# The first recurrence: a norm in pieces of 32 tokens, and the bias as a row of ones

## The reference

```python
residual = x
h = x.transpose(0, 2, 3, 1).reshape(Bsz, Hh * Ww, C)
mu = jnp.mean(h, axis=-1, keepdims=True)
var = jnp.mean((h - mu) ** 2, axis=-1, keepdims=True)
hn = (h - mu) * jax.lax.rsqrt(var + LN_EPS) * gamma + beta
z = jnp.einsum('blc,ec->ble', hn, W_in) + b_in
u = jnp.einsum('ble,se->bls', z, Bm)
def step(state, u_t):
    state = jnp.tanh(state @ A.T + u_t)
    return (state, state)
_, states = jax.lax.scan(step, init, u_tm)
y = jnp.einsum('bls,es->ble', states, Cm) + z * D
out = jnp.einsum('ble,ce->blc', y, W_out) + b_out
return out + residual
```

## Time and profile before

| | us |
|---|---|
| median of 3 runs | 684.7 (683.07 to 684.82) |
| the profiled execution | 685.12 |
| its span | 683.3 |
| TensorE busy | 483.1 |
| ScalarE busy | 324.3 |
| VectorE busy | 300.2 |

### The profile page before, as it was taken

One profiled execution on the slowest core, in us unless ns is written; L12 is line 12 of the kernel. 1 busy time (PEld: TensorE's weight loads), 2 busy tenths in 40 slices (PEclk: granted clock), 3 DMA queues, 4 the chain that ended last, 5 costly groups with the idle time before them and its releaser, 6 DMA issues.

```text
span 683.3 us, 10793 instructions
## 1 busy us (share of the span) xinstructions
PE 483.1 (71%) x3952; PEld 267.9 (39%) x3953; DVE 300.2 (44%) x721; ACT 324.3 (47%) x1093; POOL 8.6 (1%) x11
## 2 busy tenths in 40 slices
PE   4654555556797589999856666666667799989753
PEld 2221222223563466766623333333332454446311
DVE  1184000005983678888843000000007888378533
ACT  3232333333672757777732333333347555666433
POOL 0000000000000000000000000000003000000010
PEclk9655555556999999999995555555559999999867
DMA  5000000000000000000000000000003110000000
GB/s 195 0 2 1 0 1 1 0 1 0 0 2 1 0 2 1 1 1 1 2 0 1 0 1 0 1 1 0 1 0 85 38 39 6 1 2 3 0 9 33
DMA packets 8381, 7.44 MB, mean 11 GB/s; under 512 B 3202, under 2 KB 8066, under 8 KB 8196
## 3 DMA queue, kind: packets, MB, share of 16 engines
q1 hardware_dynamic: 8324, 6.70, 3.3%
HBM read 4.99 MB, written 0.52 MB: 8 GB/s over the span
## 4 chain that ended last, share of the span: by engine, by line
PE 57%; DVE 16%; ACT 16%; issue 7%; DVEq 1%; DMA 1%; SPq 1%; ACTq 0%
PE ps L325 17%; ACT arena L343 11%; PE ps L303 4%; PE ps L308 3%; PE ps L672 2%; PE ps L879 2%; PE ps L842 2%; PE ps L659 2%; PE ps L655 2%; PE ps L858 2%; PE ps L686 2%; DVE arena L1411 2%; DVE arena L1420 2%; PE ps L846 2%; PE ps L265 2%
## 5 line engine op out<-in xcount | busy, mean ns | idle before, releaser
L325 PE MATMUL ps<-arena,wsb 16*16 16x16 f32 (+1 forms) x1024 | 131.1, 206 | 116.9 <-ACT arena L343 111.4
L343 ACT ACTIVATE arena<-ps 16x16 f32<-16x16 f32 (+1 forms) x512 | 96.0, 188 | 191.0 <-PE ps L325 191.0
L325 PEld LDWEIGHTS ps<-arena,wsb 16*16 16x16 f32 (+1 forms) x1024 | 76.2, 118 | 200.3 <-ACT arena L343 186.9
L349 DVE TENSOR_TENSOR X<-X,ps 128x128 f32<-128x128 f32 x16 | 4.6, 287 | 199.3 <-PE ps L308 199.3
L1103 ACT ACTIVATE arena<-ps,arena 128x128 f32<-128x128 f32 (+1 forms) x128 | 52.3, 418 | 31.2 <-DVE arena L1412 31.1
L1211 ACT ACTIVATE arena<-ps 128x512 f32<-128x512 f32 x72 | 40.8, 595 | 26.8 <-PE ps L846 24.3
L1560 DVE TENSOR_TENSOR arena<-arena,ps 128x512 f32<-128x512 f32 x64 | 42.0, 682 | 17.3 <-ACT arena L1211 13.5
L1411 DVE TENSOR_REDUCE arena<-ps 128x2 f32<-128x512 f32 (+1 forms) x48 | 33.0, 688 | 18.7 <-PE ps L655 11.2
L672 PE MATMUL ps<-wsb,arena 128*128 128x128 f32 x192 | 30.4, 282 | 13.5 <-DVE arena L1420 13.5
L659 PE MATMUL ps<-arena 128*128 128x256 f32 x128 | 34.8, 395 | 0.0
L1420 DVE TENSOR_TENSOR arena<-arena 128x512 f32<-128x512 f32 x48 | 33.2, 691 | 1.6
(11 more groups left out here) (277 smaller groups left out, 753.4 us busy)
## 6 DMA issues: line engine op xcount, KB each, us to landing
wsb<-weights SPq DMA_DIRECT2D x1, 2060.5 KB, 9.4
arena<-w SPq DMA_DIRECT2D x20, 64.0 KB
arena<-xn SPq DMA_DIRECT2D x9, 128.0 KB, 2.5
wsb<-weights SPq DMA_DIRECT2D x1, 549.5 KB, 4.4
X<-x SPq DMA_DIRECT2D x1, 512.0 KB, 3.4
out<-arena SPq DMA_DIRECT2D x2, 256.0 KB, 2.4
arena<-w_biases SPq DMA_DIRECT2D x20, 17.0 KB
csb<-consts SPq DMA_DIRECT2D x1, 128.0 KB, 9.2
```

The source lines that it names most:

```text
L325: nc.tensor.matmul(step_columns(k, rows, r), w_state, states[0:rows, :, :, t].rearrange("p g j -> p (g j)"), start=False, stop=True, skip_ ...
L343: nc.scalar.activation(states[0:rows, :, :, t + 1].rearrange("p g j -> p (g j)"), step_columns(t // STEP_BANK, rows, t % STEP_BANK), func) ...
```

## The change

Ahead of step 0 only the first 32 tokens of each sequence are normalised (128 columns in place of 1024), with ScalarE as before. The other seven pieces of 32 tokens are normalised during the recurrence: TensorE centres a piece with 4 products (`chunk_products`, L335 in the changed kernel) and sums squares with 4 more (L340), each behind one step, at the steps that CENTRED and VARIED list; VectorE does the rest, with 1/sigma from an integer start value and three Newton steps (L1347 to L1359), since ScalarE keeps the tanh. The bias no longer goes through VectorE: `states` gets a 17th row of ones, the state matrix a_w a 17th row that holds Bm by the bias of z (L598, L599). The skip product is made bank by bank behind the steps r = 5, 8, 11, 14 (`skip_product`, L320), one step behind the out product (L311) that it waits for, and the last piece's at r = 20, 23, 26, 29 of the last bank. The fills move from r = 17, 20, 23, 26 to 20, 23, 26, 29, in the second recurrence too. The mask tables on VectorE stand behind the seventh piece. The first layer's weights come in two DMAs.

```diff
+FILLS, OUTS, SKIPS = (20, 23, 26, 29), (4, 7, 10, 13), (5, 8, 11, 14)
+CENTRED = ((0, 1, 2, 3), (16, 17, 18, 19), (32, 33, 34, 35), (49, 50, 51, 53), (65, 66, 67, 70), (85, 86, 88, 89), (105, 108, 111, 112))
+VARIED = ((6, 7, 8, 9), (24, 25, 27, 28), (41, 44, 47, 48), (59, 60, 62, 63), (80, 81, 82, 83), (94, 95, 98, 99), (117, 118, 120, 121))
...
-            if g == G - 1:
-                mm.then_inc(s["bank out"], 1)
+            mm.then_inc(s["bank out"], 1)
+
+        def skip_product(pe, m, g):
+
+            group = slice(C * g, C * (g + 1))
+            bank, c0 = (m, P) if m < BANKS - 1 else (m - 1, 2 * P)
+            pe.wait_ge(s["bank out"], G * bank + g + 1)
+            nc.tensor.matmul(ps[group, bank, c0:c0 + P], g2[group, group], xnj[group, :, STEP_BANK * m:STEP_BANK * (m + 1)],
+                             start=True, stop=True).then_inc(s["L0 skip"], 1)
+
+        def chunk(t, m):
+
+            return t.rearrange("p (j t) -> p j t", j=J)[:, :, STEP_BANK * m:STEP_BANK * (m + 1)]
+
+        def chunk_products(pe, t):
+
+            for m in range(1, BANKS):
+                for g in range(G):
+                    group = slice(C * g, C * (g + 1))
+                    if t == CENTRED[m - 1][g]:
+                        if g == 0 and m > 2:
+                            pe.wait_ge(s["L0 chunk saved"], 2 * (m - 2))
+                        nc.tensor.matmul(ps[group, 4 + m % 2, 0:P], W("centre")[group, group], chunk(X[:], m)[group], start=True, stop=True)\
+                            .then_inc(s["L0 chunk products"], 1)
+                    if t == VARIED[m - 1][g]:
+                        if g == 0:
+                            pe.wait_ge(s["L0 chunk saved"], 2 * m - 1)
+                        nc.tensor.matmul(ps[group, 6 + m % 2, 0:P], W("block")[group, group], chunk(sq[:], m)[group], start=True, stop=True)\
+                            .then_inc(s["L0 chunk products"], 1)
...
-                if r == 0 and n == 0:
-                    pe.wait_ge(s["bank biased"], k + 1)
-                if r == 0 and n == 1:
+                if r == 0:
                     pe.wait_ge(s["bank filled"], fills(n, k, G))
...
-                nc.tensor.matmul(step_columns(k, rows, r), w_state, states[0:rows, :, :, t].rearrange("p g j -> p (g j)"),
+                nc.tensor.matmul(step_columns(k, rows, r), w_state, states[0:rows + ones, :, :, t].rearrange("p g j -> p (g j)"),
...
-                if k > 0 and r in (4, 7, 10, 13):
-                    bank_out(k - 1, (r - 4) // 3, rows, w_out)
-                if k < BANKS - 1 and r in (17, 20, 23, 26):
-                    if n == 0 and k + 1 == 6 and r == 17:
-
-                        pe.wait_ge(s["L0 skip added"], 2)
-                    if n == 1 and STEP_BANK * (k + 1) == P and r == 17:
+                if n == 0 and k == 1 and r == OUTS[0]:
+                    pe.wait_ge(s["L0 weights"], 2)
+                if k > 0 and r in OUTS:
+                    bank_out(k - 1, OUTS.index(r), rows, w_out)
+                if n == 0 and k > 0 and r in SKIPS:
+                    skip_product(pe, k - 1, SKIPS.index(r))
+                if n == 0 and k == BANKS - 1 and r in FILLS:
+                    skip_product(pe, k, FILLS.index(r))
+                if n == 0:
+                    chunk_products(pe, t)
+                if k < BANKS - 1 and r in FILLS:
+                    if n == 0 and r == FILLS[0]:
+
+                        pe.wait_ge(s["L0 chunk saved"], 2 * (k + 1 if k < 3 else min(k + 3, BANKS - 1)))
+                    if n == 1 and STEP_BANK * (k + 1) == P and r == FILLS[0]:
                         pe.wait_ge(s["F input"], 2)
-                    bank_fill(pe, n, k + 1, (r - 17) // 3, rows, w_in)
+                    bank_fill(pe, n, k + 1, FILLS.index(r), rows, w_in)
...
-            sp.dma_start(wsb[:, 0:l0], weights[:, 0:l0]).then_inc(s["L0 weights loaded"], 16)
+            norm = COL["L0_W_in"][0]
+            sp.dma_start(wsb[:, 0:norm], weights[:, 0:norm]).then_inc(s["norm weights loaded"], 16)
+            sp.dma_start(wsb[:, norm:l0], weights[:, norm:l0]).then_inc(s["L0 weights loaded"], 16)
             sp.dma_start(wsb[:, l0:], weights[:, l0:]).then_inc(s["weights loaded"], 16)
...
+            pe.wait_ge(s["x loaded"], 16)
+            pe.wait_ge(s["norm weights loaded"], 16)
+            nc.tensor.matmul(ps[:, 7, 0:P], W("centre"), chunk(X[:], 0), start=True, stop=True).then_inc(s["centred"], 2)
             pe.wait_ge(s["L0 weights loaded"], 16)
-            nc.tensor.matmul(ps[:, 4, 0:P], W("L0_W_in", E2), W("L0_BmT", E2), start=True, stop=True)
-            nc.tensor.matmul(ps[:, 4, P:2 * P], W("L0_Cm", E2), W("L0_W_outT", E2), start=True, stop=True)
             nc.tensor.matmul(ps[0:E2, 5, 0:1], W("L0_W_inT", C), W("L0_beta", C), start=True, stop=True).then_inc(s["L0 folds"], 1)
-            pe.wait_ge(s["L0 z bias"], 1)
-            nc.tensor.matmul(ps[:, 4, 2 * P:3 * P], W("L0_W_in", E2), d_wout[:], start=True, stop=True)
-            nc.tensor.matmul(ps[:, 5, 2:3], W("L0_BmT", E2), z_b[:], start=True, stop=True)
-            nc.tensor.matmul(ps[:, 5, 1:2], d_wout[:], z_b[:], start=True, stop=True).then_inc(s["L0 folds"], 1)
-
-            norm_tensor(pe, 0)
+            pe.wait_ge(s["squares"], 2)
+            nc.tensor.matmul(ps[:, 6, 0:P], W("block"), chunk(sq[:], 0), start=True, stop=True).then_inc(s["variance"], 2)
+            nc.tensor.matmul(ps[:, 4, 0:P], W("L0_W_in", E2), W("L0_BmT", E2), start=True, stop=True).then_inc(s["L0 folds"], 1)
+            pe.wait_ge(s["L0 z bias"], 2)
+            nc.tensor.matmul(ps[0:NS + 1, 3, 0:NS], W("ident", NS)[:, 0:NS + 1], W("L0_AT", NS)[:, 0:NS], start=True, stop=False)
+            nc.tensor.matmul(ps[0:NS + 1, 3, 0:NS], z_row, W("L0_BmT", E2)[:, 0:NS], start=False, stop=True).then_inc(s["L0 folds"], 1)
+            nc.tensor.matmul(ps[:, 2, 0:P], W("L0_Cm", E2), W("L0_W_outT", E2), start=True, stop=True)
+            nc.tensor.matmul(ps[:, 2, P:2 * P], W("L0_W_in", E2), d_wout[:], start=True, stop=True)
+            nc.tensor.matmul(ps[:, 2, 2 * P:2 * P + 1], d_wout[:], z_row[:, NS:], start=True, stop=True).then_inc(s["L0 folds"], 1)
             pe.wait_ge(s["L0 weights"], 1)
             pe.wait_ge(s["normalised"], 2)
             for g in range(G):
-                bank_fill(pe, 0, 0, g, NS, u_w[:])
-
-            for h in range(2):
-                nc.tensor.matmul(ps[:, 6 + h, :], g2[:], halves(xn)[h], start=True, stop=True).then_inc(s["L0 skip"], 1)
-            recur_tensor(pe, 0, NS, u_w[:], W("L0_AT", NS)[:, 0:NS], g1[0:NS, 0:C])
+                mm = nc.tensor.matmul(ps[0:NS, 0, g * P:(g + 1) * P], u_w[:, C * g:C * g + NS], chunk(xn[:], 0),
+                                      start=(g == 0), stop=True, skip_group_check=True)
+            mm.then_inc(s["bank filled"], G)
+            pe.wait_ge(s["X ready"], 1)
+            recur_tensor(pe, 0, NS, u_w[:], a_w, g1[0:NS, 0:C], ones=1)
             pe.wait_ge(s["weights loaded"], 16)
+            pe.wait_ge(s["L0 chunk saved"], 2 * (BANKS - 1) + 1)
...
-            norm_scalar(act, 0)
+            act.preload_act_table_set(EXP_LN)
+            act.wait_ge(s["centred"], 2)
+            nc.scalar.activation(chunk(sq[:], 0), ps[:, 7, 0:P].rearrange("p (j t) -> p j t", j=J), ACT.Square, scale=C ** -0.5)\
+                .then_inc(s["squares"], 2)
+            act.wait_ge(s["variance"], 2)
+            nc.scalar.activation(chunk(sq[:], 0), ps[:, 6, 0:P].rearrange("p (j t) -> p j t", j=J), ACT.Ln, bias=W("eps"))\
+                .then_inc(s["log variance"], 2)
+            act.wait_ge(s["log variance"], 2)
+            nc.scalar.activation(chunk(sq[:], 0), chunk(sq[:], 0), ACT.Exp, scale=-0.5).then_inc(s["1/sigma"], 2)
...
-            dve.wait_ge(s["x loaded"], 16)
-            nc.vector.memset(states[:, :, :, 0:1], 0.0).then_inc(s["X ready"], 1)
+            nc.vector.memset(z_row, 0.0)
+            link(nc.vector.memset(states[0:NS + 1], 1.0))
+            nc.vector.memset(states[0:NS, :, :, 0:1], 0.0).then_inc(s["X ready"], 1)
...
-
-            def bias_bank(k):
-
-                dve.wait_ge(s["bank filled"], fills(0, k, G))
-                nc.vector.tensor_scalar(ps[0:NS, k, :], ps[0:NS, k, :], u_b[0:NS], None, ALU.add).then_inc(s["bank biased"], 1)
-
-            bias_bank(0)
-            for h in range(2):
-                dve.wait_ge(s["L0 skip"], h + 1)
-                nc.vector.scalar_tensor_tensor(halves(X)[h], ps[:, 6 + h, :], o_b[:], halves(X)[h], ALU.add, ALU.add)\
-                    .then_inc(s["L0 skip added"], 1)
-            dve.wait_ge(s["L0 skip added"], 2)
-            bias_bank(1)
...
+            dve.wait_ge(s["L0 folds"], 3)
+            nc.vector.tensor_copy(a_w, ps[0:NS + 1, 3, 0:NS]).then_inc(s["L0 weights"], 1)
+            dve.wait_ge(s["1/sigma"], 2)
+            nc.vector.tensor_tensor(chunk(xn[:], 0), chunk(sq[:], 0), ps[:, 7, 0:P].rearrange("p (j t) -> p j t", j=J), ALU.mult)\
```

(34 more changed lines are left out.)

27 lines of the change are left out of this document (13 added, 14 removed).

## The result

The changed kernel took 677.07 us, median of 4 executions (676.33 to 677.42), against 684.51 for the kernel before on the same chip (683.07 to 684.82): a ratio of 0.9877, 95% interval 0.9845 to 0.9909. It is faster by 7.4 us (1.2%), where 15.2 were forecast, and outside the range of 666 to 674.5. The profiled execution took 676.94 us, its span is 675.0 (before 685.1 and 683.3).

What follows compares the result with a forecast made beforehand. The two recurrences, closed chains of steps, were taken to bound the kernel, with 22.2 us ahead and 5.1 inside. 685.1 - 11.2 - 5.1 + 1.5 + 0.3 - 0.9 = 669.7, 0.4 lower for the median: 669.3 us; range 666 to 674.5.

Steps and rivals of the forecast that it cites:

- step 64: Inside the first recurrence: step 64 no longer waits for VectorE's bias, 0.60 instead of 5.72 us, gain 5.1 us.
- VectorE's chain: Normalising pieces on VectorE during the recurrence: 13 dependent operations plus copy and squares per piece, cost 0.3 us (0 to 1.0).
- start: Ahead of the first recurrence: step 0 at 11.0 us instead of 22.2, gain 11.2 us (10.0 to 12.2).
- skip waits: Recurrence steps behind 28 waiting skip products: 0.16 us each for 7, 0.02 for 21, cost 1.5 us (0 to 8.4).
- clock: TensorE in the recurrence: a third of the 1.2 us from the upper clock level, plus lessened skip cost, gain 0.9 us.
- Rival C: Clock goes up and stays: no skip cost, 1.2 us from steps, start 1.0 earlier, 666.5 us; chance 0.13.
- From the end of the recurrence on, each stage as long as before: Sign for everything behind the first recurrence: no stage there changes its length.
- both tight places: Pieces 3 to 4 and 5 to 6, steps 59 and 94: no wait at 0.32 us per operation, 0.4 each at 0.352.
- Rival B: Skip products hold a recurrence step whole: 8.4 us in place of 1.5, no clock gain, 677 us; chance 0.10.
- D: Each of 88 new products behind steps pushes the next step by 0.21 us: costs 18.5, total 686.9; chance 0.03.
- E: Step 64's wait returns elsewhere: VectorE operations at 0.45 us, pieces late, some 8 to 10 us, 678 us; chance 0.04.

Runs made afterwards that it cites:

- e3: The kernel before with only the mask tables' loop on VectorE split around the bias of bank 2: 680.15 us, ratio 0.9913.
- e2: The changed kernel with the 28 skip products two steps behind their out product instead of one, seven chunk products a step earlier: 671.28 us, ratio 0.9815.
- e6: The kernel before with 88 already met waits added to TensorE's program, ahead of three waits it has anyway: 693.84 us, ratio 1.0112.
- e12: The changed kernel without TensorE's implied wait for the saved copy three units back, 45 instructions fewer: 674.85 us, ratio 0.9820.
- e4: The changed kernel with the 2060.5 KB transfer of the other weights issued only once the first layer's weights are there: 677.22 us, ratio 0.9896.
- e1: The changed kernel with the first layer's weights in one DMA again: 674.77 us, ratio 0.9849.
- e11: The kernel before with 88 empty waits in TensorE's program, one behind each of 88 first-recurrence steps from step 139: 694.86 us, ratio 1.0158.
- e5: The changed kernel with 168 already met waits added to TensorE's program, ahead of three waits it has anyway: 677.38 us, ratio 0.9891.
- e7: The changed kernel with later skip products, large weights after the first layer's, piece 4's first two variance products a step later, 168 empty waits: 673.14 us, ratio 0.981.
- e10: The changed kernel with later skip products, delayed large weights, later chunk 4 variances, and 160 empty waits behind recurrence steps: 674.87 us, ratio 0.9863.
- e14: The kernel before without TensorE's implied wait for the saved copy three units back, 45 instructions fewer: 685.24 us, ratio 0.9981.
- e9: The changed kernel with 160 empty waits in TensorE's program, two behind each of 80 first-recurrence steps from step 128: 680.56 us, ratio 0.9966.

## Why the prediction was wrong

Of the mechanisms it named, step 64 and VectorE's chain came as priced, the start and the skip waits were mis-sized, and the clock's gain didn't come; one cost it didn't have. Forecast against measured, in us:

| term | forecast | measured | from |
|---|---|---|---|
| start | -11.2 | -9.65 | step 0 at 12.55 |
| step 64 | -5.1 | -5.1 | ordinary step; e3 alone -5.06 |
| 28 waits of skip products | +1.5 | +3.6 | 16.88 against 16.35, e2 |
| VectorE's chain | +0.3 | +0.3 | step 60 |
| clock | -0.9 | 0 | steps 0.51 throughout |
| exit of the program | none | +4.2 | 9.75 against 5.55; e6, e12 |
| sum | -15.4 | -6.7 | medians: -7.4 |

The two sums are 8.7 apart: 4.2 of it is the exit, 2.1 the skip waits, 1.5 the start, 0.9 the clock. Without the exit the time would have lain inside the range.

**The start** failed in one number, "the second piece ends where all of it ended before, 5.7". It ended at 7.07, and by e4 and e1 it is the split together with the large transfer behind it that holds it up. The upper bound had 0.5 for this, too little. Everything behind was right within 0.2: the memset was covered, the fills took 1.89 for 1.8.

**The skip waits** were the term with the widest bounds (0 to 8.4), and I took 0.02 for 21 of the 28, because two tiles had been seen at work at once. They do work at once, but the tanh behind came only once the older product had ended. The Trainium skill (TensorE: Matmul & The Clock Gate, Part 3: Packing small matmuls) has products end in the order of the program even on different tiles; the second pair of rows above agrees with it in kind, and shows 0.11 where I had worked out 0.07 by it. For group 0 it was 0.17, where I had 0.16. So 7 x 0.17 + 21 x 0.11 = 3.5. The rows of before held no case of a long product ahead of a step product in another tile, and between the Trainium skill's rule and my reading of two tiles I chose wrongly. That the order of the ends is the reason is read from these rows; e2 shows that the wait goes when the skip product starts earlier, which the rule would have too.

**The clock** term rested on TensorE's share of busy time rising. It rose (10.30 of 16 us against 9.52), and the products stayed at the lower level's durations, 0.61 to 0.63 for a product behind a step. Rival C is out.

**The exit** was in neither the sum nor a rival. "From the end of the recurrence on, each stage as long as before" holds for every stage except the last 10 us, after the last work has been issued. In the fourteen experiments and the two kernels the length of TensorE's program sorts the ends: with 11 instructions in the last 256 (changed, e1, e2, e4, e6, e11) 9.05 to 9.75 us, with 134 to 222 (before, e3, e5, e7 to e10, e12 to e14) 5.5 to 6.2. e6 has it without the change, e12 hasn't got it with the change. In each of the six long ones, and in none of the ten others, a branch of TensorE behind the loops takes 4.7 to 5.0 us with instruction fetches beginning in it, and TensorE arrives last, 3.5 to 3.8 us behind the others. That the branch waits for these fetches is read from their times; why there are three of them isn't known.

VectorE's chain came out at its 0.3 partly by luck: it was one wait of 0.28, at step 60, where the prediction's own arithmetic gave none or 0.4 at both tight places.

Rival B had its cost in the right place and over twice too high; that its 677 is the measured time is chance, since it has neither the exit nor the late start. D and E didn't happen: the 56 chunk products cost nothing but the 0.28 at step 60, and the first bank, which has 16 of them and four fills behind its steps but no skip product, takes 16.35 as before.

## What to carry to other kernels

Ahead of an instruction on a closed chain, count not only whether a queued product starts in time but whether it ends before the chain's own; moving 28 of them one step later gave back 3.7 us. A large transfer issued right behind an urgent one can take from it (1.1 us here): let it wait. When a change lengthens an engine's program, look at the span behind the last issue as well, and at which engine arrives last at the end: here 11 instructions in the last 256 made the exit 3.5 to 4.2 us longer, and 45 implied waits less took that away.

## What the runs showed of the hardware

- With 11 instructions in TensorE's last 256, three fetches of 16 KB lie in the last 10 us, a branch of TensorE behind the loops takes 4.7 to 5.0 us in place of 0.2, and the end is 3.5 to 3.9 us longer (9.05 in e6 and 9.43 in e11 against 5.52 in e14; 9.75 in the changed kernel against 5.95 in e12).
- A wait that is already met isn't free: 0.075 us per step in front of a step product, the same for one or two of them (e9, e11), though TensorE sits idle for 0.28 ahead of a bare step.
- The 354.5 KB of weights took 4.1 to 4.2 us to land when the 2060.5 KB waited for them, and 4.8 to 5.6 with these issued 0.46 us later.
- The upper clock level came at different times in profiles of the same code ahead of step 0: L268 took 1.98 us in before and 3.06 in e14, and the recurrence began 2 us later.
- The granted clock is printed as 1.00 ahead of its first record (157.4 us here), while products ran at the lower level's durations.
- One profile can be 2.5 us short in one stage and 4 long in another against other kernels of the same code there (the table of stages); a stage's difference between two single profiles is not yet the change's.
